# Fourth layer of a four-layer attention and state-space kernel: cross scores of two heads issued together, each over its own 32 partitions

## Chip, cores and metric

The kernel runs on one core of a Trainium2 chip (trn2). The metric is the device time of one execution in microseconds; lower is better. The kernel's runs are compared by their median.

## What is computed

The input x is 16 sequences of 112 tokens with 256 features, the context 16 sequences of 375 tokens with 256 features, all in fp32. Four layers follow one another, and each of them ends with attention to the context. Only the fourth matters here: a Mamba-2 block (state-space scan), then cross-attention with 8 heads of 32 features.

```python
def _L3_xattn_ref(x, encoder_out, encoder_padding_mask, ...):
    # D, N_HEADS, D_INNER, D_STATE, D_CONV = 256, 8, 512, 128, 4
    def _cross_attention(x, enc, pad_mask, ln_w, ln_b, Wq, Wk, Wv, Wo):
        dh = D // N_HEADS
        xn = _ln(x, ln_w, ln_b)
        q = (xn @ Wq).reshape(b, Lq, N_HEADS, dh)
        k = (enc @ Wk).reshape(b, Lk, N_HEADS, dh)
        v = (enc @ Wv).reshape(b, Lk, N_HEADS, dh)
        scores = jnp.einsum('bqhd,bkhd->bhqk', q, k) * np.float32(1.0 / np.sqrt(dh))
        scores = jnp.where(pad_mask[:, None, None, :], jnp.float32(-1000000000.0), scores)
        p = jax.nn.softmax(scores, axis=-1)
        ctx = jnp.einsum('bhqk,bkhd->bqhd', p, v).reshape(b, Lq, D)
        return resid + ctx @ Wo
    h = _mamba2_block(x, ...)
    return _cross_attention(h, encoder_out, ...)
```

## The kernel before

**Turns.** Every layer runs in eight turns, each with two of the 16 sequences (`PAIR`). In the fourth layer (`layer3`) a turn issues the cross-attention of its two sequences, 16 heads numbered 0 to 15 (the *items* of the `Part` named `cross`), and beside them, in small portions, the state-space block, the keys, values and queries of the *next* turn (`state(i, s)` on each engine). There is a prologue that does only the state work for turn 0, a loop over seven turns with state work, and a last turn, written out behind the loop, that has none.

**Steps.** `lagged` sets the order of the program on each engine by hand. At step n TensorE issues the transposes of head n-3 (`turns`, line 546), the scores of head n (`scores`, line 538), at n = 7, 11, 15 and 19 the value products of the four heads up to n-4 (`values`, line 568), and then the state work of step n. VectorE does the maximum of head n (`maxima`, line 665: it adds the padding bias to the scores in PSUM, writes the sum to the tile `l_p` and takes the row maximum), then the reciprocal and scaling of head n-1 (lines 677 and 590), then its state work. ScalarE copies the transposes of head n-3 out of PSUM (line 614), takes the exponentials of head n (line 631), then does its state work. All engines run in program order, and semaphores join them.

**Scores.** A head has 32 features, of 128 partitions on which the keys of four heads lie (`ckT[:, j, hh // 4, :]`, 375 columns). The queries lie in `qz`, in the room shared with other layers (`weights_of_layers_and` in the profile): for each of four heads a copy of 112 columns, with the head's 32 partitions filled and the other 96 zero. The product contracts all 128 partitions, so the other three heads' keys meet zeros. It is one fp32 product of 112 by 375, which the hardware does in two passes, each with its own weight load and record in the profile.

**Banks.** The scores go to two PSUM banks in turn (`banks[0:2]`), the transposes to two more, the outputs of the value products to one, the products of the state work to a ring of three (`P`). Head n's scores wait until its bank is free, which is when VectorE has done head n-2's maximum. `TR` is the ring of transposes, `p_free` makes the maximum of head n wait for the transposes of head n-4 (four slots of `l_p`).

**Value products.** Each head gives 32 rows of output, so the four heads of a burst go to four groups of 32 columns of the array: `bank[a * ph.dh:(a + 1) * ph.dh, ...]` for a = 0 to 3, in a loop over three tiles of 125 keys with the four heads inside it.

**State work around the change (TensorE).** Steps 0 and 1: convolution channels (line 161, three products of 256 channels) and time steps; 2 and 3: gate rows; 6 and 8: decays spread over the partitions (line 2767, waiting for GpSimd, line 2656); 9: transposes of the inner rows (2752) and the product of B and C (2759); 10: two blocks of keys (161); 12 and 13: sums over the weighted decays (2774); 14 and 15: values; 16: transposes of the gated rows (2783), a block of keys; 17: state output (161); 18, 19 and behind: keys, values, transposes, queries. VectorE's share: step 2 and 4 to 6 convolution taps (2978), 3 the softplus series (2991 to 3000), 7 and 9 scans (3012), 8 the silu (3058), 10 keys (3005) and the mean square of the next x (2958), 11 and 12 weighted decays (3020), 13 and 14 gating (3027, 3029, 2958), 15 scaling of the gated rows (3072).

Of the kernel before, what the change touches and what calls it, by code (L numbers as in the profile page):

```python
# [9 lines left out]
NB, T, D, S2 = 16, 112, 256, 375  # L10
# [416 lines left out]
class Part:  # L427


    def __init__(self, name, items, dh, rows, q, k, val, ready, val_ready, place, out, bias=None, grouped=False, sides=2, tiles=CT,  # L430
                 turned_by="act", emptied_by="dve", scaled_by="dve", ring=None):
        self.name, self.items, self.dh, self.rows, self.q, self.k, self.val, self.ready = name, items, dh, rows, q, k, val, ready
        self.val_ready, self.place, self.out, self.bias, self.grouped, self.sides, self.ring = val_ready, place, out, bias, grouped, sides, ring
        self.turned_by, self.emptied_by, self.scaled_by = turned_by, emptied_by, scaled_by
        self.keys, self.tiles = (T, 1) if grouped else (CP, tiles)
        self.n = G if grouped else 1
        self.by_probs = bias is not None
        self.scored_by = "dve" if self.by_probs else "act"
# [15 lines left out]
class Columns(Attention):  # L454
# [74 lines left out]
    def tensor(self, pe, i, parts, ident, between=None):  # L529
        S, TR, p, pT = self.S, self.TR, self.p, self.pT  # L530

        def scores(ph, k):
            m = ph.first + k
            for sem, count in S.free(i, m, *ph.ready(k)):
                pe.wait_ge(sem, count)
            width = ph.keys * ph.tiles
            for g in range(ph.n):
                last = pe.matmul(S.bank(m)[:ph.rows, g * width:(g + 1) * width], ph.q(k, g), ph.k(k, g), start=True, stop=True)  # L538
            last.then_inc(S.full.sem, 1)

# [1957 lines left out]
def layer3(nc, c, x_in, context, x_out, small, row_dt, row_A, row_D, conv_w, pad_words):  # L2498
# [7 lines left out]
    with ctx:  # L2506
# [44 lines left out]
        def cross_at(k):  # L2551
            return k // H3, k % H3
# [9 lines left out]
        def cross_q(k, g):  # L2562
            j, hh = cross_at(k)
            return qz[:, hh // 4, hh % 4, j * T:(j + 1) * T]

        def cross_value(k, g, t):
            j, hh = cross_at(k)
            return cv[:, j, t, hh * DH3:(hh + 1) * DH3]

        cross = Part("c", PAIR * H3, DH3, T, cross_q, lambda k, g: ckT[:, cross_at(k)[0], cross_at(k)[1] // 4, :], cross_value, cross_ready, cross_values_ready,  # L2570
                     lambda k: (f"cO{cross_at(k)[0]}", cross_at(k)[1] // 4 * T), lambda k: OT_of[:, cross_at(k)[0], :], bias=lambda k: padded[:T, :],
                     sides=4, emptied_by="act")
        LAST = cross.items + LAG_VALUES
# [742 lines left out]
```

## Time and profile before

| | us |
|---|---|
| runs | 3820.96, 3871.56, 3872.68 |
| median | 3871.56 |
| profiled execution, its own time | 3822.77 |
| its span, first to last instruction | 3821.0 |
| mean granted TensorE clock in it | 0.963 of full speed |

The profile is one execution. Its times are microseconds from the start of the span; the durations of records are in ns. The clock is given as a share of the full speed of 2.4 GHz; 0.5 is 1.2 GHz. In a timeline, instructions of one line that follow one another are merged into one row: start, duration of the group, engine, line, operation, output<-inputs, partitions*columns of the weights, shape of the moving operand, count, and in brackets the idle time before it with what ended it. TensorE's ends are modelled, so neighbouring groups overlap; the difference between starts is the time that a group holds the engine.

### The profile page before, as it was taken

To read this page: it belongs to the slowest core of one execution; us is meant where nothing else is said; L and a number is where in the kernel's file an instruction comes from. 1 tells how busy PE (TensorE), PEld (TensorE's weight loads), DVE (VectorE), ACT (ScalarE), POOL (GpSimd) and SP (SyncE) were. 2 spreads that over 40 slices of the span, in tenths; PEclk is the share of its full clock that TensorE was granted. 3 is DMA by queue.
4 is the path that set the end of the run, shared out by engine and by line. 5 is a ranking of instruction groups with operands and counts; after the bars stand their busy time and mean duration, and the time that the engine had idled before them with its cause. 6 is when DMAs were issued, how large, how long until landed. Compare 5 with 4: busy or idle time off the path is not lost. (4 is left out here: it accounts for less than half of the span.)

```text
span 3821.0 us, 67697 instructions
## 1 busy us (share of the span) xinstructions
PE 3584.9 (94%) x21748; PEld 2729.5 (71%) x21748; DVE 2020.9 (53%) x6215; ACT 1746.1 (46%) x4893; POOL 402.0 (11%) x488
## 2 busy tenths in 40 slices
PE   8999999999989999999997999999999997888888
PEld 6778778887867888888775666666676674565565
DVE  4644555464445555556554445445445445657656
ACT  3544545454443333334333545555555453344444
POOL 2101101110101111101101000000000001211111
PEclk9999999999999999999998999999999998898999
DMA  5000000000040000000001000000000000000000
GB/s 199 4 11 14 9 9 12 14 4 12 6 134 12 13 13 13 7 6 13 13 3 49 8 15 8 8 14 8 8 14 8 8 10 14 11 26 13 13 26 5
DMA packets 58462, 75.11 MB, mean 20 GB/s; under 512 B 6752, under 2 KB 55584, under 8 KB 57024
## 3 DMA queue, kind: packets, MB, share of 16 engines
q1 hardware_dynamic: 58176, 71.45, 5.9%
q8 instruction: 160, 2.62, 0.3%
q14 instruction: 126, 1.03, 0.1%
HBM read 64.04 MB, written 7.40 MB: 19 GB/s over the span
## 5 line engine op out<-in xcount | busy, mean ns | idle before, releaser
L161 PE MATMUL l_bank<-l_xT,weights_of_layers_and 128*128 128x224 f32 x2816 | 619.5, 374 | 17.2 <-ACT l_xT L1161 8.0
L161 PEld LDWEIGHTS l_bank<-l_xT,weights_of_layers_and 128*128 128x128 f32 x2816 | 550.1, 201 | 54.0 <-ACT l_xT L1161 8.7
L614 ACT ACTIVATE l_pT<-l_bank 125x336 f32<-125x336 f32 (+2 forms) x736 | 347.1, 472 | 341.0 <-PE l_bank L546 330.3
L546 PEld LDWEIGHTS l_bank<-identity,l_p 112*125 112x125 f32 (+2 forms) x2336 | 334.8, 178 | 184.6 <-issue 96.8
L546 PE MATMUL l_bank<-identity,l_p 112*125 112x112 f32 (+2 forms) x2336 | 390.0, 279 | 21.6 <-DVE l_p L590 18.2
L631 ACT ACTIVATE l_p<-l_p,l_nm 112x375 f32<-112x375 f32 x384 | 233.4, 608 | 284.9 <-DVE l_nm L665 283.8
L161 PE MATMUL l_bank<-l_cT,weights_of_layers_and 128*128 128x375 f32 x832 | 306.3, 495 | 4.7 <-DVE l_z L1811 3.7
L161 PE MATMUL l_bank<-weights_of_layers_and,l_cT 128*125 128x256 f32 (+2 forms) x960 | 301.0, 451 | 0.2
L728 POOL TENSOR_TENSOR l_ve<-l_mv,eps 112x2 f32<-112x2 f32 (+1 forms) x89 | 17.3, 195 | 2548.7 <-DVE l_mv L722 2548.7
L590 DVE TENSOR_SCALAR l_p<-l_p,l_rs 112x375 f32<-112x375 f32 (+1 forms) x608 | 255.1, 420 | 21.7
L568 PEld LDWEIGHTS l_bank<-l_pT,l_cv 125*64 125x64 f32 (+1 forms) x3648 | 163.6, 131 | 138.7 <-issue 98.7
L627 ACT ACTIVATE l_p<-l_p,l_nm 112x112 f32<-112x112 f32 x512 | 192.2, 377 | 148.6 <-DVE l_nm L661 134.1
L373 ACT ACTIVATE l_p<-l_bank,l_nm 112x375 f32<-112x375 f32 x256 | 145.8, 573 | 247.2 <-DVE l_nm L401 247.2
L665 DVE CUSTOM_DVE_ANT_0 l_p<-l_bank,weights_of_layers_and 112x375 f32<-112x375 f32 x256 | 139.1, 544 | 202.6 <-issue 122.1
L161 PEld LDWEIGHTS l_bank<-l_cT,weights_of_layers_and 128*128 128x128 f32 x832 | 155.4, 195 | 105.6 <-issue 17.9
L568 PE MATMUL l_bank<-l_pT,l_cv 125*64 125x112 f32 (+2 forms) x3648 | 226.0, 273 | 2.0 <-ACT l_pT L614 1.8
L303 PE MATMUL l_bank<-l_ckT,l_qz 128*112 128x375 f32 x512 | 216.9, 510 | 4.5 <-DVE l_qz L1806 3.9
L161 PEld LDWEIGHTS l_bank<-weights_of_layers_and,l_cT 128*125 128x125 f32 x960 | 161.1, 189 | 80.5 <-issue 52.4
L313 PEld LDWEIGHTS l_bank<-identity,l_p 112*125 112x125 f32 (+1 forms) x1024 | 154.4, 179 | 76.0 <-ACT l_p L373 11.2
L538 PE MATMUL l_bank<-l_ckT,l_qz 128*112 128x375 f32 x512 | 203.2, 480 | 0.2
L401 DVE TENSOR_REDUCE l_nm<-l_bank 112x1 f32<-112x375 f32 x256 | 139.1, 546 | 99.4 <-PE l_bank L303 97.7
L538 PE MATMUL l_bank<-l_ckz,l_qT 128*128 128x375 f32 x448 | 177.0, 480 | 0.0
(253 smaller groups left out, 6118.6 us busy)
## 6 DMA issues: line engine op xcount, KB each, us to landing
l_cT<-in_ctx_turned SPq DMA_DIRECT2D x32, 375.0 KB, 3.4
l_cx<-in_ctx SPq DMA_DIRECT2D x16, 375.0 KB
context_rows<-in_ctx_reversed SPq DMA_DIRECT2D x16, 375.0 KB
tokens<-x_after_layer SPq DMA_DIRECT2D x25, 224.0 KB, 2.6
x_after_layer<-l_z SPq DMA_DIRECT2D x24, 224.0 KB, 2.4
weights_of_layers_and<-bias_lines_kept SPq DMA_DIRECT2D x1, 2625.0 KB, 16.3
weights_of_layers_and<-in_L_xattn_w_fused SPq DMA_DIRECT2D x1, 2048.0 KB, 10.7
weights_of_layers_and<-in_L_xattn_w_ff SPq DMA_DIRECT2D x1, 2048.0 KB, 12.7
```

Source lines behind the costliest of these rows:

```text
L161: last = pe.matmul(out, left, right, start=(k == 0), stop=(k == len(pairs) - 1))
L303: last = pe.matmul(bank[:T, 0:S2], ph.q(j, r), ph.k(j, r), start=True, stop=True)
L313: last = pe.transpose(bank[:ph.keys, g * T:(g + 1) * T], p[:, m % PD, g * ph.keys:(g + 1) * ph.keys], ident[:T, :T])
L373: act.activation(p[:, m % PD, 0:S2], S.bank(m)[:T, 0:S2], ACT.Exp, bias=nm[:, ph.col0 + k:ph.col0 + k + 1]).then_inc(S.emptier(m).sem, 1)
L401: dve.tensor_reduce(nm[:, ph.col0 + k:ph.col0 + k + 1], S.bank(m)[:T, 0:S2], AX.X, ALU.max, negate=True).then_inc(self.neg_max.sem, 1)
L538: last = pe.matmul(S.bank(m)[:ph.rows, g * width:(g + 1) * width], ph.q(k, g), ph.k(k, g), start=True, stop=True)
L546: last = pe.transpose(TR.bank(m)[:ph.keys, g * ph.rows:(g + 1) * ph.rows], p[:ph.rows, m % self.p_slots, g * ph.keys:(g + 1) * ph.keys], i ...
L568: last = pe.matmul(bank[a * ph.dh:(a + 1) * ph.dh, column:column + w], ph.val(n, 0, t), pT[:ph.keys, (ph.first + n) % self.pT_slots, t * w ...
L590: eng.tensor_scalar(own, own, self.rs[:r, c:c + 1], None, ALU.mult).then_inc(self.scaled["dve"].sem, 1)
L614: return act.activation(out, src, ACT.Copy)
L627: last = act.activation(own, own, ACT.Exp, bias=nm[:r, c + g:c + g + 1], accum_out=sums[:r, c + g:c + g + 1])
L631: act.activation(own, own, ACT.Exp, bias=nm[:r, c:c + 1], scale=-1.0, accum_out=sums[:r, c:c + 1]).then_inc(self.probs.sem, 1)
```

## The change

`Part` gets an argument `abreast`, 2 for the fourth layer's cross part and 1 for all others. `scores` does nothing for an odd head there; for an even one it first waits for the banks of both heads, then issues both products, each with its own increment of the semaphore. The queries and keys are cut to the 32 partitions of the head (`32 * (hh % 4)` and 32 on), so the weights are 32 by 112 and the moving keys 32 by 375; the partitions of two neighbouring heads are two different row groups of the array. What `qz` and `ckT` hold and how they are filled stays.

```diff
--- before.py
+++ after.py
@@ -428,7 +428,8 @@
 
 
     def __init__(self, name, items, dh, rows, q, k, val, ready, val_ready, place, out, bias=None, grouped=False, sides=2, tiles=CT,
-                 turned_by="act", emptied_by="dve", scaled_by="dve", ring=None):
+                 turned_by="act", emptied_by="dve", scaled_by="dve", ring=None, abreast=1):
+        self.abreast = abreast
         self.name, self.items, self.dh, self.rows, self.q, self.k, self.val, self.ready = name, items, dh, rows, q, k, val, ready
         self.val_ready, self.place, self.out, self.bias, self.grouped, self.sides, self.ring = val_ready, place, out, bias, grouped, sides, ring
         self.turned_by, self.emptied_by, self.scaled_by = turned_by, emptied_by, scaled_by
@@ -530,13 +531,16 @@
         S, TR, p, pT = self.S, self.TR, self.p, self.pT
 
         def scores(ph, k):
-            m = ph.first + k
-            for sem, count in S.free(i, m, *ph.ready(k)):
-                pe.wait_ge(sem, count)
-            width = ph.keys * ph.tiles
-            for g in range(ph.n):
-                last = pe.matmul(S.bank(m)[:ph.rows, g * width:(g + 1) * width], ph.q(k, g), ph.k(k, g), start=True, stop=True)
-            last.then_inc(S.full.sem, 1)
+            if k % ph.abreast:
+                return
+            width, own = ph.keys * ph.tiles, range(k, k + ph.abreast)
+            for n in own:
+                for sem, count in S.free(i, ph.first + n, *ph.ready(n)):
+                    pe.wait_ge(sem, count)
+            for n in own:
+                for g in range(ph.n):
+                    last = pe.matmul(S.bank(ph.first + n)[:ph.rows, g * width:(g + 1) * width], ph.q(n, g), ph.k(n, g), start=True, stop=True)
+                last.then_inc(S.full.sem, 1)
 
         def turns(ph, k):
             m = ph.first + k
@@ -2561,15 +2565,19 @@
 
         def cross_q(k, g):
             j, hh = cross_at(k)
-            return qz[:, hh // 4, hh % 4, j * T:(j + 1) * T]
+            return qz[32 * (hh % 4):32 * (hh % 4) + 32, hh // 4, hh % 4, j * T:(j + 1) * T]
+
+        def cross_k(k, g):
+            j, hh = cross_at(k)
+            return ckT[32 * (hh % 4):32 * (hh % 4) + 32, j, hh // 4, :]
 
         def cross_value(k, g, t):
             j, hh = cross_at(k)
             return cv[:, j, t, hh * DH3:(hh + 1) * DH3]
 
-        cross = Part("c", PAIR * H3, DH3, T, cross_q, lambda k, g: ckT[:, cross_at(k)[0], cross_at(k)[1] // 4, :], cross_value, cross_ready, cross_values_ready,
+        cross = Part("c", PAIR * H3, DH3, T, cross_q, cross_k, cross_value, cross_ready, cross_values_ready,
                      lambda k: (f"cO{cross_at(k)[0]}", cross_at(k)[1] // 4 * T), lambda k: OT_of[:, cross_at(k)[0], :], bias=lambda k: padded[:T, :],
-                     sides=4, emptied_by="act")
+                     sides=4, emptied_by="act", abreast=2)
         LAST = cross.items + LAG_VALUES
         state_jobs = {-1: [("xT", "act")], 0: [("b0", "act"), ("b1", "act")], 1: [("b2", "act"), ("dt", "dve")], 2: [("z0", "dve")], 3: [("z1", "dve")],
                       6: [("dc00", "dve"), ("dc01", "dve")], 8: [("dc10", "dve"), ("dc11", "dve")], 9: [("xh0", "act"), ("xh1", "act"), ("g", "act")],
```

The order changes on TensorE alone. Line numbers from 431 on are higher by 4 in the changed kernel (538 is 542, 546 is 550, 568 is 572), those in `layer3` by 8 behind the queries. First, TensorE at the start of a turn, steps 0 to 2; `l3_bank0` and `l3_bank1` are the banks of the scores, `REGISTER_ALU` rows make the count of a wait. Before:

```order
L538 MATMUL l3_bank0<-l3_ckT,weights_of_layers_0_and_2 112x375
L770 REGISTER_ALU x2
L161 MATMUL l3_bank6<-l3_xT,weights_of_layers_1_and_3 128x224 x4
L770 REGISTER_ALU
L161 MATMUL l3_bank7<-l3_xT,weights_of_layers_1_and_3 128x224 x4
L535 REGISTER_ALU
L538 MATMUL l3_bank1<-l3_ckT,weights_of_layers_0_and_2 112x375
L161 MATMUL l3_bank5<-l3_xT,weights_of_layers_1_and_3 128x224 x4
L2724 REGISTER_ALU
L161 MATMUL l3_bank6<-weights_of_layers_1_and_3,l3_xT 112x8 x4
L535 REGISTER_ALU
L538 MATMUL l3_bank0<-l3_ckT,weights_of_layers_0_and_2 112x375
```

After:

```order
L542 MATMUL l3_bank0<-l3_ckT,weights_of_layers_0_and_2 112x375
L542 MATMUL l3_bank1<-l3_ckT,weights_of_layers_0_and_2 112x375
L774 REGISTER_ALU x2
L161 MATMUL l3_bank6<-l3_xT,weights_of_layers_1_and_3 128x224 x4
L774 REGISTER_ALU
L161 MATMUL l3_bank7<-l3_xT,weights_of_layers_1_and_3 128x224 x4
L161 MATMUL l3_bank5<-l3_xT,weights_of_layers_1_and_3 128x224 x4
L2732 REGISTER_ALU
L161 MATMUL l3_bank6<-weights_of_layers_1_and_3,l3_xT 112x8 x4
L539 REGISTER_ALU x2
L542 MATMUL l3_bank0<-l3_ckT,weights_of_layers_0_and_2 112x375
L542 MATMUL l3_bank1<-l3_ckT,weights_of_layers_0_and_2 112x375
```

Head 1's scores now stand before the channels (line 161), head 3's before the gate rows. Second, TensorE from the end of step 5 to the first spread decays of step 6. Before:

```order
L546 MATMUL l3_bank3<-identity,l3_p 125x112 x3
L535 REGISTER_ALU
L538 MATMUL l3_bank0<-l3_ckT,weights_of_layers_0_and_2 112x375
L2766 REGISTER_ALU
L2766 ISA
L2767 MATMUL l3_bank6<-weights_of_layers_0_and_2,l3_ones 112x448
```

After:

```order
L550 MATMUL l3_bank3<-identity,l3_p 125x112 x3
L539 REGISTER_ALU x2
L542 MATMUL l3_bank0<-l3_ckT,weights_of_layers_0_and_2 112x375
L542 MATMUL l3_bank1<-l3_ckT,weights_of_layers_0_and_2 112x375
L2774 REGISTER_ALU
L2774 ISA
L2775 MATMUL l3_bank6<-weights_of_layers_0_and_2,l3_ones 112x448
```

Head 7's scores stand right behind head 6's, with both waits ahead of the spread decays. Third, TensorE from step 11 to step 13, head 11's scores first. Before:

```order
L538 MATMUL l3_bank1<-l3_ckT,weights_of_layers_0_and_2 112x375
L568 MATMUL l3_bank4<-l3_pT,l3_cv 32x112 x12
L546 MATMUL l3_bank3<-identity,l3_p 125x112 x3
L535 REGISTER_ALU
L538 MATMUL l3_bank0<-l3_ckT,weights_of_layers_0_and_2 112x375
L2772 REGISTER_ALU
L2772 ISA
L2774 MATMUL l3_bank6<-weights_of_layers_0_and_2 112x64 x8
L546 MATMUL l3_bank2<-identity,l3_p 125x112 x3
L535 REGISTER_ALU
L538 MATMUL l3_bank1<-l3_ckT,weights_of_layers_0_and_2 112x375
L2772 REGISTER_ALU x2
```

After:

```order
L550 MATMUL l3_bank2<-identity,l3_p 125x112 x3
L572 MATMUL l3_bank4<-l3_pT,l3_cv 32x112 x12
L550 MATMUL l3_bank3<-identity,l3_p 125x112 x3
L539 REGISTER_ALU x2
L542 MATMUL l3_bank0<-l3_ckT,weights_of_layers_0_and_2 112x375
L542 MATMUL l3_bank1<-l3_ckT,weights_of_layers_0_and_2 112x375
L2780 REGISTER_ALU
L2780 ISA
L2782 MATMUL l3_bank6<-weights_of_layers_0_and_2 112x64 x8
L550 MATMUL l3_bank2<-identity,l3_p 125x112 x3
L2780 REGISTER_ALU x2
```

No scores stand in step 11 and 13 any more; head 13's come ahead of the first weighted decays (line 2774, now 2782).

## Rows read from the trace of the kernel before

**Rows 1.** The page's first part: each engine's busy time, share of the span, instructions.

```profile
PE 3584.9 (94%) x21748; PEld 2729.5 (71%) x21748; DVE 2020.9 (53%) x6215; ACT 1746.1 (46%) x4893; POOL 402.0 (11%) x488
```

**Rows 2.** Stretches by turn: start:end, length; busy PE, PEld, DVE, ACT, POOL; granted clock; DMA.

```profile
3282.10:3356.50 74.40, 64.26 (x359) 44.13 (x357) 47.16 (x162) 34.16 (x90) 12.77 (x14) 0.86 0.05 16
...
3428.50:3503.20 74.70, 64.16 (x359) 44.16 (x358) 47.41 (x162) 34.16 (x90) 13.51 (x15) 0.86 0.06 17
...
3719.70:3791.00 71.30, 59.55 (x355) 41.08 (x353) 47.40 (x162) 34.04 (x90) 13.16 (x14) 0.93 0.02 5
3791.00:3821.00 30.00, 23.09 (x184) 13.49 (x184) 17.16 (x82) 17.61 (x50) 0.00 (x0) 1.00 0.05 14
```

**Rows 3.** Line 538 in the fourth layer: shortest/middle/longest record in ns, first and last start.

```profile
L538 PEld LDWEIGHTS l_bank<-l_ckT,weights_of_layers_and x256: 173/178/312, 3282.0 to 3811.2; 128*112 128x112 f32 x128
L538 PE MATMUL l_bank<-l_ckT,weights_of_layers_and x256: 477/481/835, 3282.1 to 3811.5; 128*112 128x375 f32 x128
```

**Rows 4.** Timeline of TensorE, turn from 3719.7: start and duration in us, merged group, wait.

```profile
3732.09 0.80 PE L538 MATMUL l_bank<-l_ckT,weights_of_layers_and 128*112 128x375 f32 x2
3732.73 0.48 PE L546 MATMUL l_bank<-identity,l_p 112*125 112x112 f32 x3
```

**Rows 5.** Timeline of VectorE, the same turn: maxima of heads 2, 5 and 7.

```profile
3727.70 0.06 DVE L710 MEMSET l_scratch<- 1x1 f32 x1 [1.79 <-PE l_bank L538]
...
3737.82 0.55 DVE L665 CUSTOM_DVE_ANT_0 l_p<-l_bank,l_padded 112x375 f32<-112x375 f32 x1
...
3746.22 0.54 DVE L665 CUSTOM_DVE_ANT_0 l_p<-l_bank,l_padded 112x375 f32<-112x375 f32 x1
```

**Rows 6.** Timeline of TensorE, the same turn, steps 6 to 9: its waits.

```profile
3735.89 0.55 PE L546 MATMUL l_bank<-identity,l_p 112*125 112x112 f32 x3 [2.05 <-DVE l_p L590]
3736.28 0.80 PE L538 MATMUL l_bank<-l_ckT,weights_of_layers_and 128*112 128x375 f32 x2
3739.02 3.33 PE L2767 MATMUL l_bank<-weights_of_layers_and,l_ones 112*112 112x448 f32 x4 [1.95 <-POOL weights_of_layers_and L2656]
...
3748.35 1.01 PE L2767 MATMUL l_bank<-weights_of_layers_and,l_ones 112*112 112x448 f32 x2 [1.68 <-DVE weights_of_layers_and L3012]
...
3751.89 0.62 PE L2752 MATMUL l_bank<-identity,weights_of_layers_and 128*112 128x128 f32 x4 [1.58 <-DVE weights_of_layers_and L3058]
```

**Rows 7.** Timeline of TensorE, the same turn, steps 10 to 12.

```profile
3756.29 1.37 PE L538 MATMUL l_bank<-l_ckT,weights_of_layers_and 128*112 128x375 f32 x2
3757.49 2.69 PE L161 MATMUL l_bank<-l_cT,weights_of_layers_and 128*128 128x375 f32 x8
...
3760.33 0.80 PE L538 MATMUL l_bank<-l_ckT,weights_of_layers_and 128*112 128x375 f32 x2
3761.06 0.78 PE L568 MATMUL l_bank<-l_pT,l_cv 125*32 125x112 f32 x24
3761.77 0.58 PE L546 MATMUL l_bank<-identity,l_p 112*125 112x112 f32 x3
```

**Rows 8.** Timeline of VectorE, the same turn: waits at steps 10 and 13.

```profile
3757.70 0.54 DVE L665 CUSTOM_DVE_ANT_0 l_p<-l_bank,l_padded 112x375 f32<-112x375 f32 x1 [2.98 <-issue]
...
3760.22 0.55 DVE L3005 TENSOR_TENSOR l_ckT<-l_bank,l_kept_keys 128x375 f32<-128x375 f32 x1 [0.71 <-PE l_bank L161]
...
3766.43 0.54 DVE L665 CUSTOM_DVE_ANT_0 l_p<-l_bank,l_padded 112x375 f32<-112x375 f32 x1 [0.81 <-issue]
```

**Rows 9.** Timeline of TensorE, the same turn: the output projection of the state part.

```profile
3777.30 3.62 PE L161 MATMUL l_bank<-weights_of_layers_and 128*112 128x256 f32 x16
```

**Rows 10.** Timeline of the last turn, VectorE and TensorE: heads 5 to 7.

```profile
3796.19 0.54 DVE L665 CUSTOM_DVE_ANT_0 l_p<-l_bank,l_padded 112x375 f32<-112x375 f32 x1
...
3796.80 0.80 PE L538 MATMUL l_bank<-l_ckT,weights_of_layers_and 128*112 128x375 f32 x2
...
3797.64 0.54 DVE L665 CUSTOM_DVE_ANT_0 l_p<-l_bank,l_padded 112x375 f32<-112x375 f32 x1 [0.37 <-issue]
...
3799.25 0.80 PE L538 MATMUL l_bank<-l_ckT,weights_of_layers_and 128*112 128x375 f32 x2
```

## Prediction

> **What bounds the kernel now.** I read the page's busy line first: TensorE's matmuls are busy for 94% of the span, the next engine, VectorE, for 53% [rows 1]. A reader would conclude that every matmul microsecond saved is a microsecond gained. The change touches only the fourth layer, though, so the second view is the table of stretches, cut at the first cross score of each of its eight turns [rows 2]. A turn takes 71.3 to 74.7 us and seven of them fill 3282.1 to 3791.0, 72.7 us on average; TensorE is busy in 59.6 to 64.3 us of each, so 11 us of every turn are waits. The eighth turn has no state work beside its heads and takes 30.0 us. The mean granted clock of a turn is 0.86 to 0.93, so part of each turn runs at the lower of the two levels (1.2 instead of 2.4 GHz), and the turns with 0.86 are the long ones.
>
> The third view is the timeline of one turn, the one from 3719.7, for TensorE and VectorE. It falls into three pieces. Up to head 2 VectorE sits idle before each head's maximum, until the scores come (1.79 us before head 2's) [rows 5]: TensorE decides. From there VectorE runs almost without a gap (softplus series, convolution taps, scans), and TensorE waits: 2.05 us before the transposes of head 3, 1.95 us for GpSimd's spread decays, 1.68 us for a scan, 1.58 us for the silu [rows 6]. From head 10 on the two alternate: VectorE waits 2.98 us for head 10's scores, 0.71 us for the second block of keys and 0.81 us for head 13's scores [rows 8], TensorE for the weighted decays and, behind head 15, for the gated rows; the projections at the turn's end are TensorE's alone.
>
> **What the scores cost.** One head's scores are two records (two passes of the fp32 product), 481 ns each in the middle; a group of two shows 0.80 us [rows 3, 4], but the next group begins 0.64 us after it (3732.09 to 3732.73), since the ends are modelled and overlap. That is 0.32 us a pass. 128 heads are 82 us of TensorE time.
>
> **Do two heads run at once?** No row of before contracts 32 partitions in another row group, so this is bounded from both sides: nothing gained, or one head of two for free, 0.64 us a pair. The nearest row is the value products: twelve fp32 products with 32 columns of weights each, to four column groups of the array. Their 24 records are over 0.71 us after they begin (3761.06 to 3761.77) [rows 7]. Sixteen full-width records of 256 columns show 3.62 us, 3.46 without the 0.16 us by which ends overlap, 0.216 us each [rows 9]; scaled to 112 columns that is 0.095 us, and 24 in a row would be 2.3 us. So four groups do run together, 3.2-fold, and both fp32 passes with them. I take full overlap for row groups too: a pair costs 0.64 us.
>
> **What the pair adds.** The array is cut differently before and after it. Scores to the next full-width group take 0.64 us, scores to the value products 0.73 us (3760.33 to 3761.06), so the change of cut is 0.09 us; behind the value products the same again, for the next group begins 0.07 us before their modelled end instead of 0.16 us [rows 4, 7]. I take 0.09 us at either end; the other bound is the weight load of 178 ns [rows 3] laid bare, 0.18 us. Value products follow on odd steps, where no pair stands now, so no change of cut is shared or saved: 0.18 us a pair, 64 pairs, 11.5 us. The net saving of TensorE time is 41.0 - 11.5 = 29.5 us, if all of it were on the path.
>
> The Trainium skill ("TensorEngine Tiling (Array Packing)", Key Properties) says that a change of tiling mode drains the engine, which speaks against the change. By that rule, the trace agrees: the 0.09 us at each end of the value products is such a drain. The page gives no time for it, so the sum stays with the rows.
>
> **The waits that move.** Head n+1's scores used to wait for head n-1's maximum one step later; now the pair of an even step n waits for both banks, and so for the maximum of head n-1. Queued behind it on TensorE is the state work of that step. At step 6 the pair needs head 5's maximum, which ends at 3738.3 (3737.82 and 0.55 us) [rows 5], where head 6's scores began at 3736.28 [rows 6]. The wait costs next to nothing: the spread decays behind it waited for GpSimd until 3739.02 anyway. A pair begun at 3738.4 ends its stay at 3739.2, 0.2 us late, and the transposes of step 9 are held by VectorE until 3751.89 whatever comes [rows 6]. At step 8 the pair needs head 7's maximum, until 3746.8 [rows 5]. It holds up the first of that step's spread decays to 3746.8 + 0.1 + 0.8 = 3747.7, but the second waits for a scan until 3748.35 as it is [rows 6]. VectorE's run hides both; without that cover they would cost about 2 us each, by which the pair comes later than head 6's scores alone did.
>
> **The sum for a turn.** Start of the turn: heads 0 and 1 cost 1.28 us before head 2's scores, now 0.64 + 0.18 = 0.82; head 2's own come 0.09 us later for the change of cut. VectorE starts its run 0.45 - 0.09 = 0.36 us earlier, and everything up to head 10 follows it. Steps 3 to 9: no score in them is on the path, 0. Step 10: the pair stands before the key projections, +0.18 us, which reach VectorE through the second block of keys [rows 7, 8]. Steps 11 to 13: TensorE waits for weighted decays both times, so the first product is 0.2 us late. But head 13's scores are ready one step early, and VectorE's 0.81 us of idle time before that maximum goes [rows 8]. It is 0.81 - 0.18 = 0.63 us ahead from there, through the gating, the root and the gated rows. TensorE, which pays for heads 14 and 15 as one, is 0.7 us ahead at step 15 and so doesn't take it back. What is late next is the gated rows' transposes, which still wait for VectorE. Behind these no scores stand, and the 0.63 us reach the next turn. Together 0.99 us a turn, seven turns: -7 us.
>
> The last turn: heads go at 2.45 us a pair (TensorE's scores at 3796.80 and 3799.25), with 0.37 us of VectorE idle [rows 10]. Now a pair waits for the maximum begun at 3796.19, ends at 3796.73; with 0.1 us to start, 0.09 us for the cut and 0.80 us to the end, the next maximum begins at 3797.75 instead of 3797.64. That is 0.1 us for each of seven pairs: +1 us.
>
> The sum is -6 us. Against the profiled execution's own 3822.77 us (span 3821.0) that is 3816.8. The runs of before are 3820.96, 3871.56 and 3872.68: the profiled one stands at the lower of two levels 51 us apart, the median at the upper. The change doesn't touch what parts them, so I forecast the median, 3871.56 - 6 = 3865.6 us. About 2% is what a measurement of this kernel can tell from no change, and this is 0.2%.
>
> **Rivals.**
> 1. *The whole saving counts.* If TensorE's 94% meant what it seems to, the 29.5 us would come out whole: 3842. For it speaks [rows 1]; against it the waits of [rows 6, 8], which grow by what TensorE saves. Chance 0.07.
> 2. *No overlap.* Row groups may share a path that column groups don't, such as the output side, where both heads write the same 112 partitions. Then a pair takes 1.28 + 0.18 us. At the start of the turn the first pair costs 0.18 us more and head 2 comes 0.09 us later, +0.3. At step 10 the second head stands before the key projections too, at the lower clock there (the group is left after 1.20 us, 3756.29 to 3757.49 [rows 7]): the keys are 1.4 us late, of which the wait before head 13's maximum gives 0.8 back, +0.6. That is 0.9 us a turn, +6, and +1 in the last: 3879. For it speaks that no row shows row groups together, against it that column groups do it 3.2-fold. Chance 0.15.
> 3. *Slower through the clock.* The place is steps 4 to 10. TensorE does half the score work there and waits longer in one piece (to 3738.4 at step 6, to 3746.8 at step 8). Its clock is at the lower level already after the waits before step 10: head 10's scores show 1.37 us instead of 0.80 [rows 4, 7]. If the lower level lasts longer, it reaches the key projections behind them, which show 2.69 us now and would take up to twice that. The price from rows: a turn at 0.86 takes 74.7 us, one at 0.93 71.3 [rows 2]. Were all seven at 0.86, they would be 7 x (74.7 - 72.7) = 14 us longer: with -6 that is 8 us slower, 3880. It decides from the point where an average turn loses more than 1 us to it, a third of the distance between the two kinds. Chance 0.20.
>
> Forecast as summed: 0.53. The rest, 0.05, is for what I haven't thought of. No case leaves 2% on either side by itself: the largest gain worked out is 0.8%, the largest loss 0.2%. Faster by over 2%: 0.02; within: 0.95; slower: 0.03. The range must hold the two levels of the runs, 3817 and 3866 for the forecast, since three runs may have their median at either; with rival 1's and the clock's own spread it goes from 3804 to 3884.
>
> **What would show it.** In the profile of after, the two heads' records should start within some ns of each other in two rounds, and a group of four records should show about 0.8 us and be left 0.73 us after its start. Idle before head 13's maximum should be near nothing, VectorE's run (head 2's maximum) should begin 7.7 us after the turn's first score instead of 8.1, and the seven turns should take 71.7 us on average with the granted clocks as before. Four records in 1.3 us or more would mean rival 2; turns with a granted clock below 0.86, or all near it, rival 3; turns of 69 us, rival 1. A median outside 3804 to 3884 means that some step above is wrong, not just a size.

## The result and the profile after

| | before | after |
|---|---|---|
| runs | 3820.96, 3821.9, 3871.56, 3872.68 | 3865.76, 3914.68, 3914.82, 3920.13 |
| median | 3846.73 | 3914.75 |
| profiled execution | 3822.77 | 3914.82 |
| span; mean granted clock | 3821.0; 0.963 | 3913.0; 0.929 |
| first cross score of the fourth layer at | 3282.1 | 3332.5 |
| from there to the end of the span | 538.9 | 580.5 |

The ratio of after to before is 1.0169, with a 95% interval of 1.0098 to 1.024. The kernel is slower, where 0.2% faster was forecast; whether by 2% the interval leaves open. The forecast was 3865.6 us, and the median of 3914.75 lies outside the range of 3804 to 3884.

Part of the 92 us between the two profiled executions doesn't belong to the change. Both kernels run at two levels, 49 to 51 us apart. The profiled execution of before is at its lower level, that of after at its upper. What parts the two levels is a stretch in another layer. After:

```profile
1183.00:1289.00 106.00, 106.00 (x421) 88.11 (x421) 43.88 (x96) 24.01 (x53) 0.00 (x0) 0.50 0.00 1
```

Before, the same stretch:

```profile
1183.00:1289.00 106.00, 101.11 (x652) 86.28 (x651) 55.74 (x138) 42.13 (x98) 11.82 (x9) 0.95 0.03 8
```

The columns are those of [rows 2]: stretch and length, busy time and records of PE, PEld, DVE, ACT and POOL, granted clock, share of the DMA engines, GB/s. In after TensorE is busy for the whole 106 us at the lower clock and gets through 421 records instead of 652. That is why the first cross score comes 50 us later. A run further down, of a kernel with other scores (pairs over 32 rows for four heads only), has the same piece at 1179 to 1285 us. Level by level, the change costs 3865.8 - 3821.4 = 44 us at the lower and 3914.8 - 3872.1 = 43 us at the upper, 1.1%. The ratio of 1.0169 is larger because three of the four runs of after, but two of the four of before, were at the upper level. From here on the *stretch* is the measure: first cross score of the fourth layer to the end of the span. It doesn't contain the other layer, and is 41.6 us longer in the changed kernel. Two more profiles show how well it repeats (runs 9 and 10): 539.0 and 580.5 us.

The page's first part still says 94% for TensorE, as in [rows 1], with 101 us more of it busy:

```profile
PE 3685.7 (94%) x21748; PEld 2803.2 (72%) x21748; DVE 2027.6 (52%) x6215; ACT 1743.6 (45%) x4893; POOL 401.3 (10%) x488
```

The table of stretches by turn answers to [rows 2]:

```profile
3332.50:3410.40 77.90, 67.84 (x357) 46.36 (x356) 47.84 (x162) 33.61 (x90) 12.72 (x14) 0.78 0.05 15
...
3567.10:3645.60 78.50, 67.60 (x359) 46.20 (x358) 47.60 (x162) 33.73 (x90) 13.37 (x15) 0.80 0.06 16
...
3720.60:3794.00 73.40, 64.59 (x360) 44.70 (x358) 47.97 (x162) 33.62 (x90) 13.49 (x15) 0.81 0.06 17
3794.00:3870.50 76.50, 65.32 (x353) 44.43 (x352) 47.60 (x162) 33.74 (x90) 12.88 (x14) 0.82 0.02 5
3870.50:3913.00 42.50, 35.18 (x184) 20.62 (x184) 17.12 (x82) 17.81 (x50) 0.00 (x0) 0.53 0.03 9
```

The turns with state work take 73.3 to 78.5 us, 76.9 on average instead of 72.7. Their clock is 0.78 to 0.82 instead of 0.86 to 0.93. The last turn is the clearest: 42.5 us instead of 30.0, and the clock at 0.53 instead of 1.00.

The scores themselves do what the change says. Line 542, the former 538 (columns as in [rows 3]):

```profile
L542 PEld LDWEIGHTS l_bank<-l_ckT,weights_of_layers_and x256: 167/171/308, 3332.5 to 3896.8; 32*112 32x112 f32 x128
L542 PE MATMUL l_bank<-l_ckT,weights_of_layers_and x256: 472/565/965, 3332.5 to 3897.5; 32*112 32x375 f32 x128
```

And TensorE's timeline of the turn from 3720.6, columns as in [rows 4]:

```profile
3732.07 0.89 PE L542 MATMUL l_bank<-l_ckT,weights_of_layers_and 32*112 32x375 f32 x4
3732.89 0.58 PE L550 MATMUL l_bank<-identity,l_p 112*125 112x112 f32 x3
...
3738.56 1.59 PE L542 MATMUL l_bank<-l_ckT,weights_of_layers_and 32*112 32x375 f32 x4 [1.70 <-DVE l_nm L669]
3740.08 3.33 PE L2775 MATMUL l_bank<-weights_of_layers_and,l_ones 112*112 112x448 f32 x4
...
3762.84 2.75 PE L2782 MATMUL l_bank<-weights_of_layers_and 112*112 112x64 f32 x16 [0.71 <-DVE weights_of_layers_and L3028]
3765.38 0.92 PE L550 MATMUL l_bank<-identity,l_p 112*125 112x112 f32 x3
3766.09 3.12 PE L2782 MATMUL l_bank<-weights_of_layers_and 112*112 112x64 f32 x16
3769.00 0.92 PE L550 MATMUL l_bank<-identity,l_p 112*125 112x112 f32 x3
3769.84 1.60 PE L542 MATMUL l_bank<-l_ckT,weights_of_layers_and 32*112 32x375 f32 x4
```

Four records, two heads, hold TensorE from 3732.07 to 3732.89, 0.82 us, where one head held it for 0.64 [rows 4]. That is the predicted 0.64 + 0.18. The pair at step 6 waits 1.70 us for a maximum, as forecast. What wasn't forecast stands at 3762.84: the sums over the weighted decays (two groups of 16 records) show 2.75 and 3.12 us, and the pair and the transposes around them also take nearly twice their time. The same two groups in the turn of before:

```profile
3763.60 1.79 PE L2774 MATMUL l_bank<-weights_of_layers_and 112*112 112x64 f32 x16 [0.61 <-DVE weights_of_layers_and L3020]
...
3766.22 1.70 PE L2774 MATMUL l_bank<-weights_of_layers_and 112*112 112x64 f32 x16
```

VectorE's timeline shows what becomes of the gain:

```profile
3728.08 0.55 DVE L669 CUSTOM_DVE_ANT_0 l_p<-l_bank,l_padded 112x375 f32<-112x375 f32 x1
...
3764.78 0.54 DVE L669 CUSTOM_DVE_ANT_0 l_p<-l_bank,l_padded 112x375 f32<-112x375 f32 x1
...
3771.48 0.54 DVE L669 CUSTOM_DVE_ANT_0 l_p<-l_bank,l_padded 112x375 f32<-112x375 f32 x1 [3.56 <-issue]
```

Head 2's maximum starts 7.5 us after the turn's first score (8.1 before), and head 13's wait of 0.81 us [rows 8] is gone. But head 14's maximum, which had no wait, now stands 3.56 us for scores, because the products ahead of them run at the lower clock.

### The profile page after: what moved, and what is told of

The parts are those of the page before. It is cut to its first block and busy times, and to the rows that moved or that the text cites. A ratio compares the mean times of both kernels' runs of the same rounds, so it can differ in the third digit from the quotient of the medians.

```text
span 3913.0 us, 67704 instructions
## 1 busy us (share of the span) xinstructions
PE 3685.7 (94%) x21748; PEld 2803.2 (72%) x21748; DVE 2027.6 (52%) x6215; ACT 1743.6 (45%) x4893; POOL 401.3 (10%) x488
## 5 line engine op out<-in xcount | busy, mean ns | idle before, releaser
L550 PEld LDWEIGHTS l_bank<-identity,l_p 112*125 112x125 f32 (+2 forms) x2336 | 346.3, 184 | 194.3 <-issue 98.8
L550 PE MATMUL l_bank<-identity,l_p 112*125 112x112 f32 (+2 forms) x2336 | 403.8, 286 | 25.1 <-DVE l_p L594 20.8
L161 PE MATMUL l_bank<-weights_of_layers_and,l_cT 128*125 128x256 f32 (+2 forms) x960 | 311.3, 464 | 0.2
L303 PE MATMUL l_bank<-l_ckT,l_qz 128*112 128x375 f32 x512 | 236.6, 551 | 4.5 <-DVE l_qz L1810 3.9
L313 PEld LDWEIGHTS l_bank<-identity,l_p 112*125 112x125 f32 (+1 forms) x1024 | 168.0, 194 | 86.1 <-issue 19.5
L542 PE MATMUL l_bank<-l_ckT,l_qz 128*112 128x375 f32 x512 | 203.2, 481 | 0.2
L335 PEld LDWEIGHTS l_bank<-l_cv,l_pT 125*112 125x112 f32 x1536 | 189.2, 194 | 2.5 <-issue 2.2
```

Of the source, the lines that this page charges most:

```text
L161: last = pe.matmul(out, left, right, start=(k == 0), stop=(k == len(pairs) - 1))
L303: last = pe.matmul(bank[:T, 0:S2], ph.q(j, r), ph.k(j, r), start=True, stop=True)
L313: last = pe.transpose(bank[:ph.keys, g * T:(g + 1) * T], p[:, m % PD, g * ph.keys:(g + 1) * ph.keys], ident[:T, :T])
L335: last = pe.matmul(bank[:T, g * w:(g + 1) * w], pT[:ph.keys, m % PD, t * T:(t + 1) * T], ph.val(j, r, t), start=(t == 0), stop=(t == ph.ti ...
L542: last = pe.matmul(S.bank(ph.first + n)[:ph.rows, g * width:(g + 1) * width], ph.q(n, g), ph.k(n, g), start=True, stop=True)
L550: last = pe.transpose(TR.bank(m)[:ph.keys, g * ph.rows:(g + 1) * ph.rows], p[:ph.rows, m % self.p_slots, g * ph.keys:(g + 1) * ph.keys], i ...
```

## The experiments

What is open is what lowers the clock: the order with its double wait, the overlap of two products, the changes of cut (the array is set for 32-row products and back), or the 32 rows themselves. Eight kernels take one of these at a time; a ninth is the version that they point to, and two runs repeat before and after. In the short diffs, + is against the changed kernel.

**Run 1, two heads issued together over all 128 partitions.**

```diff
-            return qz[32 * (hh % 4):32 * (hh % 4) + 32, hh // 4, hh % 4, j * T:(j + 1) * T]
+            return qz[:, hh // 4, hh % 4, j * T:(j + 1) * T]
-            return ckT[32 * (hh % 4):32 * (hh % 4) + 32, j, hh // 4, :]
+            return ckT[:, j, hh // 4, :]
```

> The pair is issued together and both banks are waited for, as in the changed kernel, but each product contracts all 128 partitions against the zero-filled queries, as before. Measured by the stretch from the first cross score to the end of the span (538.9 us before, 580.5 in the changed kernel). Theory A (the clock falls because the score products run on 32 rows, two at a time, and so less of the array's time is filled): the stretch stays within 10 us of 538.9 and the granted clock of the seven turns between 0.86 and 0.93. Theory B (the waits for both banks lengthen TensorE's pauses, and these lower the clock): 570 to 590 us, clock 0.78 to 0.82, the last turn about 42 us.

Measured: the stretch is 531.8 us, 7 less than before. First the seven turns with state work, then the last turn:

```profile
3280.90:3781.60 500.70, 425.01 (x2491) 301.70 (x2489) 331.41 (x1134) 236.14 (x630) 93.17 (x97) 0.93 0.05 16
3781.60:3812.70 31.10, 24.31 (x184) 15.81 (x184) 17.25 (x82) 17.22 (x50) 0.00 (x0) 0.95 0.04 12
```

The clock is 0.93 and 0.95. The double wait is there, 1.99 us at step 6:

```profile
3728.14 2.33 PE L542 MATMUL l_bank<-l_ckT,weights_of_layers_and 128*112 128x375 f32 x4 [1.99 <-DVE l_nm L669]
3730.26 2.59 PE L2775 MATMUL l_bank<-weights_of_layers_and,l_ones 112*112 112x448 f32 x4
```

It costs nothing, as the spread decays behind it run at full clock. VectorE waits neither for head 13 nor for head 14 (no brackets):

```profile
3756.90 0.55 DVE L669 CUSTOM_DVE_ANT_0 l_p<-l_bank,l_padded 112x375 f32<-112x375 f32 x1
3759.97 0.54 DVE L669 CUSTOM_DVE_ANT_0 l_p<-l_bank,l_padded 112x375 f32<-112x375 f32 x1
```

Theory B, the waits, falls. The seven turns take 500.7 us instead of 508.9, and 1.1 us is lost in the last turn.

This gain isn't the one summed in the prediction. The seven turns of before take 74.4, 72.0, 74.7, 71.9, 73.1, 71.5 and 71.3 us, at clocks of 0.86, 0.93, 0.86, 0.93, 0.91, 0.93 and 0.93. Those of run 1 take 73.8, 69.4, 71.1, 71.2, 71.8, 71.8 and 71.6 us, at 0.88, 0.93, 0.95, 0.95, 0.93, 0.93 and 0.93. Of the 8.2 us, more than 5 are won in the first, third and fifth turn, where the clock of before is lowest, and 2.6 in the second. The last two, at 0.93 in both kernels, are 0.3 us longer each in run 1. In whole runs the gain is smaller as well: the medians at the lower and the upper level are 2.3 and 1.5 us below those of before.

**Run 2, one head at a time over its 32 partitions** (`abreast=2` left out).

> One head at a time, in the order and with the waits of before, but over its own 32 partitions: no two products at once, 128 changes of cut. Theory A in its first form (what counts is that a product fills few rows of the array, overlapped or not): the clock falls as in the changed kernel, to about 0.80, and the stretch is 580 us or more, since nothing is saved by overlap. Theory A in its second form (what counts is how long TensorE streams, so only overlap lowers it): clock 0.86 to 0.93, and the stretch is 539 plus the changes of cut that lie on the path, 8 of 16 heads x 0.18 us x 8 turns = 12 us, so about 550. Theory B: as the second form, about 550.

Measured: 624.0 us, 85 us more than before, although order and waits are those of before:

```profile
3282.60:3856.40 573.80, 527.84 (x2491) 338.10 (x2489) 336.41 (x1134) 240.44 (x630) 92.37 (x97) 0.79 0.05 14
3856.40:3906.70 50.30, 44.56 (x184) 23.18 (x184) 17.56 (x82) 17.98 (x50) 0.00 (x0) 0.54 0.03 8
```

There is no overlap here, so the second form of theory A falls too: TensorE streams as long as ever. In the last turn it is busy 44.6 of 50.3 us, 89%, and runs at the lower clock nearly throughout; before it was busy 23.1 of 30.0 us, 77%, at full clock [rows 2]. The Trainium skill ("TensorE: Matmul & The Clock Gate", "What's actually happening") says that the clock is set by how busy the engine has been. Taken as the busy share of a profile this doesn't hold here, and the measurement decides: the engine that is busier by the profile got the lower clock. The lower clock itself raises that share, since the same 184 records take 44.6 us instead of 23.1, so the share can't tell why the clock fell; but 89% didn't bring it back either. What the run leaves open is whether the rows or the changes of cut do it, since there are 128 heads with two changes each.

**Run 3, a full-width product ahead of each pair.**

```diff
+            if ph.abreast == 2:
+                pe.matmul(S.bank(ph.first + k)[:ph.rows, 0:width], ph.full_q(k), ph.full_k(k), start=True, stop=True)
             for n in own:
```

(`full_q` and `full_k` are the even head's queries and keys over 128 partitions.)

> The changed kernel with one more product ahead of each pair: the even head's scores over all 128 partitions, into its own bank, which the pair then overwrites. TensorE streams for as long as before again, while order, waits and row groups stay. Theory A: the clock comes back to 0.86 to 0.93 and the stretch to 540 to 555 us, although 64 products (0.64 us each, 41 us of TensorE time) were added. Theory B: the waits are as long, clock about 0.80, 580 us or more.

Measured: 568.7 us, 12 less than after, although work was added:

```profile
3282.40:3809.50 527.10, 461.36 (x2603) 297.40 (x2601) 331.26 (x1134) 239.66 (x630) 92.37 (x97) 0.90 0.05 15
3809.50:3851.20 41.70, 33.10 (x200) 17.34 (x200) 17.11 (x82) 17.38 (x50) 0.00 (x0) 0.78 0.03 9
```

The clock of the seven turns comes back from 0.80 to 0.90, as theory A says, while all changes of cut and all 32-row pairs are still there. The run adds full-width products and time in which TensorE streams, both at once; runs 2, 5 and 7 tell the two apart. The time was missed (540 to 555 expected): I had given the 64 added products no place on the path, but they lengthen the seven turns (527.1 us) and even more the last one, 41.7 us at 0.78, where no state work hides them.

**Run 4, the last turn as before.**

```diff
             def turn(i, coming):
                 beside(i, -1, coming)
+                cross.abreast = 2 if coming else 1
                 A.tensor(pe, i, [cross], c.ident, lambda s: beside(i, s, coming))
```

(with the full 128 partitions where `abreast` is 1)

> The changed kernel, but the last turn, which has no state work, issues its scores as before, one head at a time over 128 partitions. Both theories: the last turn goes from 42.5 us back to 30 and its clock from 0.53 to 1.00, the seven other turns stay at 73 to 79 us, so the stretch is about 568 us. If the last turn stays near 42 us, its clock is set by what happened in the turns before it.

Measured: 568.2 us:

```profile
3282.60:3820.40 537.80, 466.15 (x2490) 319.56 (x2489) 334.23 (x1134) 235.99 (x630) 92.59 (x97) 0.80 0.05 14
3820.40:3850.80 30.40, 23.57 (x184) 13.63 (x184) 17.17 (x82) 17.61 (x50) 0.00 (x0) 0.93 0.05 14
```

The last turn is back at 30.4 us, at 0.93. Its clock doesn't hang on the turns before it, and 12 of the 41.6 us are its own.

**Run 5, one head at a time over 64 partitions** (its own 32 and 32 of zeros).

```diff
+            return qz[64 * (hh % 4 // 2):64 * (hh % 4 // 2) + 64, hh // 4, hh % 4, j * T:(j + 1) * T]
+            return ckT[64 * (hh % 4 // 2):64 * (hh % 4 // 2) + 64, j, hh // 4, :]
```

> One head at a time, order and waits of before, each product over 64 partitions (the head's own 32 and 32 of zeros). The array is cut for it as often as in the run with 32 rows, 128 times. If the rows that a product fills set the clock: between before and the 32-row run, granted clock of the turns 0.82 to 0.90, last turn 35 to 45 us at 0.65 to 0.85, stretch 560 to 600 us. If the changes of cut set it: as the 32-row run, 0.77 to 0.81 and 50 us in the last turn, stretch 615 to 630.

Measured: 589.7 us, between before and run 2, with as many changes of cut as run 2:

```profile
3283.80:3822.20 538.40, 489.56 (x2489) 313.42 (x2488) 336.52 (x1134) 240.40 (x630) 92.40 (x97) 0.85 0.05 14
3822.20:3873.40 51.20, 46.18 (x184) 23.96 (x184) 17.70 (x82) 18.03 (x50) 0.00 (x0) 0.52 0.03 9
```

The seven turns fit the rows theory (0.85, between 0.91 and 0.79). The last turn doesn't fit what I gave for it (35 to 45 us): it is as slow as with 32 rows, 51.2 us at 0.52, with TensorE busy 90% of it.

**Run 6, one head at a time over 96 partitions**, 128 for every fourth head.

> One head at a time, order of before, over partitions 0 to 95 for three heads of four and 0 to 127 for the fourth: fewer rows filled, but, if 96 rows need no other cut of the array, no change of cut. Rows theory: the clock a little below before, stretch 539 to 555 us. Cut theory: exactly as before, 539 +- 3 us, last turn 30 us at 1.00. The scores should leave TensorE after 0.64 us and not 0.73, or the array is cut for 96 rows too.

Measured: 545.2 us:

```profile
3281.80:3795.90 514.10, 436.79 (x2491) 299.93 (x2489) 332.42 (x1134) 238.46 (x630) 93.12 (x97) 0.90 0.05 15
3795.90:3827.10 31.20, 24.62 (x184) 14.38 (x184) 17.24 (x82) 17.60 (x50) 0.00 (x0) 0.95 0.05 13
```

The distance to the next group is 0.64 us, so 96 rows need no change of cut:

```profile
3728.32 0.80 PE L542 MATMUL l_bank<-l_ckT,weights_of_layers_and 96*112 96x375 f32 x2
3728.96 1.68 PE L161 MATMUL l_bank<-l_xT,weights_of_layers_and 128*128 128x224 f32 x8
```

against 0.81 us with 32 rows in run 2:

```profile
3703.32 0.88 PE L542 MATMUL l_bank<-l_ckT,weights_of_layers_and 32*112 32x375 f32 x2
3704.13 1.97 PE L161 MATMUL l_bank<-weights_of_layers_and,l_xT 128*112 128x512 f32 x4
```

So the cut is that of before and the streaming time too (the middle record is 481 ns in both), and still the clock goes from 0.91 to 0.90 and the stretch grows by 6.3 us. The runs show it at both levels: medians of 3829.0 and 3876.0 us, against 3820.9 and 3869.1 of before in the same session. Fewer rows cost time without any change of cut.

**Run 7, pairs over 64 partitions each**, heads 0 and 2, then 1 and 3.

```diff
+            return k // H3, 4 * (k % H3 // 4) + (0, 2, 1, 3)[k % 4]
-                    for a, n in enumerate(together):
+                    for n in together:
+                        a = (0, 2, 1, 3)[n % 4] if ph.abreast == 2 else n - together[0]
```

(and the rows of run 5)

> Pairs as in the changed kernel, but each product over 64 partitions with zeros in half of them; heads 0 and 2, then 1 and 3 of every four go together, so that their 64 rows are the two halves of the array (the value products put each head back to its place). Overlap and cuts are the same as in the changed kernel, with all 128 rows filled while two run. Rows theory: the clock rises over the changed kernel's 0.80 to 0.83 to 0.90, stretch 545 to 565 us. If overlap itself (half the streaming time) or the cut lowers the clock, it stays at 0.80 and 575 to 585 us.

Measured: 535.0 us, 45.5 less than after, 10 less than I gave at best for the theory that the rows count:

```profile
3280.60:3782.20 501.60, 421.18 (x2489) 287.61 (x2488) 332.48 (x1134) 238.05 (x630) 92.76 (x97) 0.89 0.05 16
3782.20:3815.60 33.40, 24.46 (x184) 14.40 (x184) 17.11 (x82) 17.35 (x50) 0.00 (x0) 0.82 0.04 12
```

This is the run that settles it. It has the overlap, the double waits and the changes of cut of the changed kernel. Only the rows differ, 64 instead of 32 for each product, and with them the order of the four heads of a group; the two of a pair fill all 128 rows between them. The clock is 0.89, and the seven turns take 501.6 us. The last turn takes 33.4, at 0.82: without state work around them even these pairs lower it.

Run 7 also shows what the overlap is worth. The last turn with state work in run 1 (first line) and in run 7:

```profile
3710.00:3781.60 71.60, 60.24 (x355) 42.86 (x353) 47.30 (x162) 33.74 (x90) 13.11 (x14) 0.93 0.02 6
3712.20:3782.20 70.00, 58.54 (x353) 39.90 (x352) 47.25 (x162) 34.01 (x90) 13.06 (x14) 0.90 0.02 6
```

It takes 71.3 us at 0.93 before [rows 2]. The pairs with overlap are shorter although their clock is lower. The difference comes at step 10, first in run 1, then in run 7:

```profile
3746.01 2.71 PE L542 MATMUL l_bank<-l_ckT,weights_of_layers_and 128*112 128x375 f32 x4
3748.51 3.03 PE L161 MATMUL l_bank<-l_cT,weights_of_layers_and 128*128 128x375 f32 x8
3751.58 0.55 DVE L3013 TENSOR_TENSOR l_ckT<-l_bank,l_kept_keys 128x375 f32<-128x375 f32 x1 [0.72 <-PE l_bank L161]
...
3748.14 1.28 PE L542 MATMUL l_bank<-l_ckT,weights_of_layers_and 64*112 64x375 f32 x4
3749.35 2.79 PE L161 MATMUL l_bank<-l_cT,weights_of_layers_and 128*128 128x375 f32 x8
3752.18 0.55 DVE L3014 TENSOR_TENSOR l_ckT<-l_bank,l_kept_keys 128x375 f32<-128x375 f32 x1 [0.72 <-PE l_bank L161]
```

The pair holds TensorE for 2.50 us in run 1 and for 1.21 in run 7, as long as head 10 alone before (1.20 [rows 7]). VectorE takes up the second block of keys 41.6 us after the turn's first score in run 1, 40.0 in run 7 and 40.6 before. In whole runs that gain doesn't show: the medians of run 7 are 1.6 us below before's at the lower level and 1.8 above at the upper.

**Run 8, 32-row pairs for heads 0 to 3 only**, full-width pairs for the others.

```diff
+            return qz[0 if k > 3 else 32 * (hh % 4):128 if k > 3 else 32 * (hh % 4) + 32, hh // 4, hh % 4, j * T:(j + 1) * T]
+            return ckT[0 if k > 3 else 32 * (hh % 4):128 if k > 3 else 32 * (hh % 4) + 32, j, hh // 4, :]
```

> Both heads issued together everywhere; over 32 rows and overlapped only for heads 0 to 3 of each turn, where TensorE sets the pace and full-width projections follow, over all 128 partitions and so one after the other for heads 4 to 15. From the sum of the prediction: 0.36 us a turn less than the full-width pairs (531.8 us), 7 turns, so 529 us, if the clock stays at 0.93 there. If 8 of the 64 pairs' 32-row products per two turns are enough to lower it: 535 to 545 us.

Measured: 533.3 us (501.7 and 31.6), clock 0.92. The 2.5 us of gain didn't show: against run 1 the seven turns are 1.0 us longer. That the saved time and the little clock that four heads cost (0.92 against 0.93) cancel each other is likely, but not shown.

**Runs 9 and 10, before and after once more.**

> The kernel before, profiled once more, to see how far the stretch from the first cross score to the end varies by itself. Expected 538.9 +- 4 us, last turn 30 us at 1.00. If the 105 us of low clock near 1183 us show here as well, they have nothing to do with the change, and the execution is at its upper level, near 3870 us.

> The changed kernel, profiled once more. The clock theory wants the stretch at 580.5 +- 5 us and the clock of the seven turns near 0.80 whichever level the execution is at; before the first cross score it should differ from the kernel before by the 105 us of low clock or not at all.

Measured: 539.0 us in the one (3821.2 us, lower level), 580.5 in the other (3912.91 us, upper level, first cross score at 3330.7). The seven turns of after have the clock at 0.80 again. Every turn agrees within 0.1 us with the first profile of its kernel, so the profiles repeat well. They are only two of each kernel, though: the runs of before at the lower level spread from 3817.0 to 3832.3 us, and a difference of a few us between single profiles counts only where the runs of the same level have it too.

**Run 11, what the runs point to:** pairs over 128 partitions in the seven turns, single heads in the last.

```diff
+            return qz[:, hh // 4, hh % 4, j * T:(j + 1) * T]
+            return ckT[:, j, hh // 4, :]
+                cross.abreast = 2 if coming else 1
```

> Two heads issued together over all 128 partitions in the seven turns with state work, and one by one in the last turn, as before: what the experiments point to. The stretch should be the full-width pairs' 531.8 us less the 1.1 us that their last turn took over 30.0, so 531 us, 8 us less than before; in the runs' times that is 0.2%, too little for a verdict. The clock of the turns 0.88 to 0.95.

Measured: 531.4 us (500.6 and 30.8), 7.5 less than before; the runs' median is 3843.3 us, the ratio 0.9986 with an interval of 0.9926 to 1.0045, so no difference from before can be told by it. Of the ten runs the five at the lower level have their median at 3817.1, of before's thirteen of the same session six at 3826.1. That would fit the profile, but at the upper level it is 3867.2 against 3868.0, and in the two earlier sessions before's lower level had its median at 3820.9. A gain of some us is possible and not shown. Run 1 with 0.9959 (0.9896 to 1.0022) stands no worse. Both are faster than the changed kernel.

The single heads and the pairs in one table (us and granted clock). The last column is the median of the runs less that of before in the same session, at the lower and at the upper level; some of these medians are of a single run (after at the lower level, runs 2 and 5 at the upper).

| rows of a product | heads | stretch | seven turns | last turn | whole runs |
|---|---|---|---|---|---|
| 128 (before) | one by one | 538.9 | 508.9, 0.91 | 30.0, 1.00 | |
| 96 (run 6) | one by one | 545.2 | 514.1, 0.90 | 31.2, 0.95 | +8.1, +6.9 |
| 64 (run 5) | one by one | 589.7 | 538.4, 0.85 | 51.2, 0.52 | +52.9, +53.2 |
| 32 (run 2) | one by one | 624.0 | 573.8, 0.79 | 50.3, 0.54 | +87.6, +91.3 |
| 128 (run 1) | pair, in turn | 531.8 | 500.7, 0.93 | 31.1, 0.95 | -2.3, -1.5 |
| 64 (run 7) | pair, together | 535.0 | 501.6, 0.89 | 33.4, 0.82 | -1.6, +1.8 |
| 32 (after) | pair, together | 580.5 | 538.0, 0.80 | 42.5, 0.53 | +44.3, +42.7 |

## Why the prediction was wrong

**Overlap and its price: right.** The pair takes 0.82 us, as summed; two row groups do run together, which no row of before showed. Rival 2 is out.

**The waits that move: right.** At step 6 the pair waits, in the run with full clock it delays nothing.

**The sum for a turn: right in size, in part by luck.** It gave -7 us for seven turns and +1 for the last. Run 7, with the same order, overlap and changes of cut at a clock near that of before, has -7.3 us (501.6 against 508.9), and the last turn +3.4. Two of its terms were off. Head 2's maximum comes 7.5 us after the turn's first score instead of 8.1, a gain of 0.6 and not 0.36, and 7.7 us in run 1, so most of it is had without any overlap. At step 10 I had the keys 0.18 us late; in run 7 they are 0.6 us early, and 1.0 us late in run 1. So the overlap does reach the path there, but nothing like its 41 us comes out of it. Run 1 reaches -8.2 us without overlap, mostly through turns in which its clock is higher, so the totals alone don't tell which term earned what. How the 7.3 us divide among order, overlap and clock stays open.

**The term left at nothing: this is the step that failed.** The sum of -6 us let every product run at the clock it had in the rows of before. Rival 3 named the clock, with a chance of 0.20, and was wrong in its cause and its size. Its cause was longer pauses of TensorE at steps 4 to 10. Run 1 has these pauses, of 1.99 us, and its clock is higher than before. Its price was 14 us, taken from the turns at 0.86, the lowest that before shows; the changed kernel is at 0.80, below every row I had, and its seven turns are 29 us longer than before, 36 us longer than those of run 7. And it left out the last turn, where before's clock is 1.00 and nothing seemed to threaten it: 12.5 us. The rows' own share is the changed kernel against run 7, which differs only in the rows and in the order of four heads: 36.4 + 9.1 = 45.5 us. With it, -6 becomes +39.5, and 41.6 was measured.

**The range** was too narrow for the same reason: its upper end was the clock's price from the rows of before, not from a kernel whose products fill a quarter of the rows. I had bounded the new operation's duration from both sides, but not what it does to the clock of its neighbours.

**Level of the median.** I forecast for the upper level, where two of three runs of before stood; with the fourth run the median was between them. The roughly 50 us between the levels are larger than the effect of the change.

## What to carry to other kernels

A product over few partitions isn't just a cheaper or an equal product: the clock for everything around such products can fall, and the busy share won't show it. Here the scores were less than a fifth of TensorE's work (128 x 0.64 = 82 of 454 busy us in the stretch before). Zeros in the unused partitions cost nothing that the trace shows, and keep the clock. If row groups are to run together, let the products of a pair fill the array between them; here that made up for the loss, and no more. And if two changes come in one edit (here the new order with the overlap, good for 4 us in the profile and for nothing clear in the runs, and the 32 rows, bad for 45), run each by itself.

## What the hardware showed unexpectedly

The clock goes with the rows that a product contracts, also where the rows left out hold only zeros: 0.91, 0.90, 0.85 and 0.79 for 128, 96, 64 and 32 rows in the seven turns, with the order of before. From 128 to 96 rows the time that a product holds TensorE is unchanged too (0.64 us); with 64 and 32 it is 0.81 us, by the changes of cut. The engine was busy 89 to 90% of the last turn at the lower clock in runs 2 and 5, and 77% at the full clock before. What the chip measures to set it, these runs don't show.

One stretch of about 105 us in another layer, from 1183 us on, is at the lower clock in some executions and not in others of one and the same kernel. The three profiled executions at the upper level have it (the changed kernel twice, run 8 once), the ten at the lower level don't, and the levels are about 50 us apart. TensorE is busy for all of it and still stays at the lower clock. What starts it was not tried.
